# Down products of an adaLN block: eight block products or seven, with the left factors prepared by three engines

## The reference

```python
h = _layernorm(x) * (1 + ca) + sa
x = x + ga * attention(h)                 # linear attention, 16 heads, outside the change
h = _layernorm(x) * (1 + cb) + sb         # x: (2, 2048, 512)
w = lut[idx]                              # gate, up: (1376, 512); down: (512, 1376)
x = x + gb * (silu(h @ gate.T) * (h @ up.T)) @ down.T
```

## Time and profile before

| what | value |
|---|---|
| median of 3 runs | 1165.8 us (1163.17 to 1166.24) |
| span of the profiled execution | 1162.8 us |
| nearest run shown, taken as the profiled execution's own time | 1163.2 us |
| TensorE busy | 1127.7 us, 97% |
| VectorE, ScalarE, GpSimd busy | 705.3, 435.6, 358.1 us |
| last gate and up product to the end of the span | 927.96 to 1162.8 us |

### The profile page before, as it was taken

One profiled execution on the slowest core, in us unless ns is written; L12 is line 12 of the kernel. 1 busy time (PEld: TensorE's weight loads), 2 busy tenths in 40 slices (PEclk: granted clock), 3 DMA queues, 4 the chain that ended last, 5 costly groups with the idle time before them and its releaser, 6 DMA issues.

```text
span 1162.8 us, 16680 instructions
## 1 busy us (share of the span) xinstructions
PE 1127.7 (97%) x6692; PEld 531.1 (46%) x6718; DVE 705.3 (61%) x1035; ACT 435.6 (37%) x729; POOL 358.1 (31%) x331
## 2 busy tenths in 40 slices
PE   4899999999999999999999999999999999999998
PEld 2344444454444444445444444444454444444443
DVE  4788988776779677996768979677432211111111
ACT  4668788776645251424323324233142200000000
POOL 1000100002126283547525637356332211111111
PEclk9999999999999999999999999999999999999999
DMA  7940233113204541312213213031121325445441
GB/s 268 322 135 1 87 109 110 38 37 109 74 1 143 182 145 74 109 73 78 82 35 118 72 72 118 35 118 43 64 92 48 147 104 179 172 173 176 177 154 59
DMA packets 52236, 125.93 MB, mean 108 GB/s; under 512 B 5216, under 2 KB 15456, under 8 KB 47040
## 3 DMA queue, kind: packets, MB, share of 16 engines
q1 hardware_dynamic: 52160, 124.87, 30.9%
HBM read 77.15 MB, written 47.71 MB: 107 GB/s over the span
## 4 chain that ended last, share of the span: by engine, by line
PE 83%; DVE 7%; issue 4%; ACT 3%; POOL 1%; DMA 1%; SPq 0%; POOLq 0%; DVEq 0%; ACTq 0%
PE bank L1232 26%; PE bank L1234 25%; PE bank L1233 25%; PE bank L1240 2%; DVE look_buf L995 2%; PE bank L1384 1%; DVE w_ffn L995 1%; DMA w_ffn<-in_wmod 1%; PE bank L1302 1%; PE bank L1366 1%; PE bank L1345 1%; DVE h L901 1%; ACT h L617 1%; ACT shared L649 1%; DVE shared L1014 0%
## 5 line engine op out<-in xcount | busy, mean ns | idle before, releaser
L1232 PE MATMUL bank<-h,w_ffn 128*128 128x512 f16 (+1 forms) x528 | 200.6, 380 | 0.2 <-POOL h L553 0.2
L1233 PE MATMUL bank<-h,w_ffn 128*128 128x512 f16 (+1 forms) x528 | 200.3, 379 | 0.0
L1234 PE MATMUL bank<-h,w_ffn 128*128 128x512 f16 (+1 forms) x528 | 200.3, 379 | 0.0
L573 POOL TENSOR_TENSOR shared<-hid_f,shared 128x512 f16<-128x512 f32 (+1 forms) x88 | 114.1, 1296 | 273.5 <-ACT shared L780 273.4
L780 ACT ACTIVATE shared<-hid_f 128x512 f16<-128x512 f32 (+1 forms) x88 | 55.4, 630 | 259.7 <-DVE hid_f L1157 251.8
L1164 DVE SCALAR_TENSOR_TENSOR shared<-bank,sc,gb_row 128x512 f32<-128x512 f32 x32 | 24.0, 751 | 205.1 <-PE bank L1234 205.1
L1157 DVE SCALAR_TENSOR_TENSOR hid_f<-bank,sc,shared 128x512 f32<-128x512 f32 (+1 forms) x88 | 65.8, 747 | 121.5 <-issue 82.4
L1232 PE MATMUL bank<-w_ffn 128*128 128x512 f16 x320 | 121.5, 380 | 0.0
L1234 PE MATMUL bank<-w_ffn 128*128 128x512 f16 x320 | 121.3, 379 | 0.0
L1233 PE MATMUL bank<-w_ffn 128*128 128x512 f16 x320 | 121.3, 379 | 0.0
L1232 PE MATMUL bank<-arena,h 128*128 128x512 f16 x256 | 98.3, 384 | 5.6 <-issue 2.5
(11 more groups left out here) (225 smaller groups left out, 1922.8 us busy)
## 6 DMA issues: line engine op xcount, KB each, us to landing
hid_dram<-shared SPq DMA_DIRECT2D x80, 256.0 KB, 2.0
w_ffn<-hid_dram SPq DMA_DIRECT2D x8, 2560.0 KB, 9.5
xg<-in_x SPq DMA_DIRECT2D x16, 1024.0 KB, 7.2
qp_dram<-qp SPq DMA_DIRECT2D x8, 1024.0 KB, 4.9
x_dram<-xg SPq DMA_DIRECT2D x8, 1024.0 KB, 4.0
xg<-x_dram SPq DMA_DIRECT2D x8, 1024.0 KB, 4.8
out<-xg SPq DMA_DIRECT2D x7, 1024.0 KB, 11.4
qp<-qp_dram SPq DMA_DIRECT2D x6, 1024.0 KB, 5.2
```

Source lines behind the costliest of these rows:

```text
L573: pool.tensor_tensor(hid[0:m, e % HIDS, 1], hid_f[0:m, e % 2], hid[0:m, e % HIDS, 0], ALU.subtract).then_inc(hid_done, 1)
L1232: pe.matmul(dst, a_hi, b_hi, start=first, stop=False)
L1233: pe.matmul(dst, a_hi, b_lo, start=False, stop=False)
L1234: last = pe.matmul(dst, a_lo, b_hi, start=False, stop=end)
```

## The change

The down product is made in 16 units of 256 rows. In each, the first 10 chunks and the two halves of 128 rows form a 2 by 2 scheme of blocks (A11, A12, A21, A22, each 5 chunks of 128 by 128), the weights another (5 chunks by 256 columns). In place of 8 block products there are 7 (PRODUCTS), of sums and differences of blocks: on the left S1 = A21 + A22, S2 = S1 - A11, S3 = A11 - A21, S4 = A12 - S2, on the right four T blocks made once. Chunk 11 is added plainly (`rest`).

Gated values go to DRAM in f32. GpSimd makes the four left sums of a unit (`left_sums`), ScalarE all high halves (`left_hi`, `last_hi`), VectorE all low halves (`sum_lo`, `raw_lo`, `last_lo`). ScalarE copies three partial results out of PSUM (`hold`), VectorE combines them (`left_u3`, `out_row`), scales (`out_scale`), and GpSimd adds to `xg` (`add_rows`). In the last step of stage B, VectorE makes the T blocks (`right_sums`, `right_lows`), ScalarE their high halves (`t_hi`), GpSimd the planes of three B blocks and of chunk 11. `hid_hi`, `hid_lo`, `unpack`, `y_tile` go. The core of the diff (constants for scales, views of buffers and semaphore names are left out):

```diff
+HALF_K = (FC - 1) // 2
+HALF_N = HID // 2
+UNIT = 2 * P
+DOWN_UNITS = BATCHES * SEQ // UNIT
...
+PRODUCTS = ((S_A11, S_B11), (S_S1, S_T1), (S_S2, S_T2), (S_A12, S_B21), (S_S3, S_T3), (S_S4, S_B22), (S_A22, S_T4))
+LEFT_PARTS = (S_A11, S_S1, S_S2, S_A12, S_S3, S_S4, S_A22)
...
-        hid = part(shared, 4 * HID, F16, HIDS, 2, GROUP)
+        hid = part(shared, 4 * HID, F32, HIDS, GROUP)
...
+            def hid_load(u):
+                g, i, cols = u // 2, u % 2, slice(u % 2 * UNIT, u % 2 * UNIT + UNIT)
...
+                if u >= 2:
+                    sp.wait_ge(raw_low, 4 * (u - 1))
+                    sp.wait_ge(left_summed, 4 * (u - 1))
+                sp.dma_start(hid_raw[i][:, 0:FC - 1], hid_dram[g][:, 0:FC - 1, cols]).then_inc(hid_in[i], 16)
+                sp.dma_start(hid_raw[i][0:TAIL, FC - 1], hid_dram[g][0:TAIL, FC - 1, cols]).then_inc(hid_in[i], 16)
...
                     elif i == 7:
+                        sp.wait_ge(tf_done, 4 * HALF_K)
+                        sp.wait_ge(b_planes, 3 * HALF_K + 1)
                         hid_load(0)
+                        hid_load(1)
...
+                for u in (2 * g + 2, 2 * g + 3):
+                    if u < DOWN_UNITS:
+                        hid_load(u)
+                if 1 <= g < GROUPS - 1:
+                    sp.wait_ge(stored[1 - par], 16 * ((g - 1) // 2 + 1))
+                    sp.dma_start(flat(xg[:, 1 - par]), x1_dram[g + 1]).then_inc(x1_in[1 - par], 16)
...
+            def b_plane(dst, j, m, cols):
...
+                pool.tensor_copy(dst, down_w[0:m, j, cols].rearrange("p n h -> p h n")).then_inc(b_planes, 1)
+            def right_planes(jj):
+                if jj == 0:
+                    wait_apart(pool, look, len(UNITS) * STEPS)
+                    wait_apart(pool, up_done, SLOT[(GROUPS - 1, 0)] + 1)
+                    b_plane(wt_last[0:TAIL], FC - 1, TAIL, slice(0, HID))
+                b_plane(wt[S_B11][:, jj], jj, P, slice(0, HALF_N))
+                b_plane(wt[S_B21][:, jj], jj + HALF_K, P, slice(0, HALF_N))
+                b_plane(wt[S_B22][:, jj], jj + HALF_K, P, slice(HALF_N, HID))
+            def left_sums(u):
...
+                a11, a12, a21, a22 = r[:, k1, 0:P], r[:, k2, 0:P], r[:, k1, P:UNIT], r[:, k2, P:UNIT]
+                pool.wait_ge(hid_in[u % 2], 32 * (u // 2 + 1))
+                if u:
+                    pool.wait_ge(sum_low, 4 * u)
+                pool.tensor_tensor(left_sum[0], a21, a22, ALU.add).then_inc(left_summed, 1)
+                pool.tensor_tensor(left_sum[2], a11, a21, ALU.subtract).then_inc(left_summed, 1)
+                pool.wait_ge(left_summed, 4 * u + 1)
+                pool.tensor_tensor(left_sum[1], left_sum[0], a11, ALU.subtract).then_inc(left_summed, 1)
+                pool.wait_ge(left_summed, 4 * u + 3)
+                pool.tensor_tensor(left_sum[3], a12, left_sum[1], ALU.subtract).then_inc(left_summed, 1)
+            def add_rows(u, i):
+                g, t = u // 2, 2 * (u % 2) + i
...
+                pool.wait_ge(y_scaled, 2 * u + i + 1)
+                pool.tensor_tensor(xg[:, g % 2, t], xg[:, g % 2, t], y_t[:, i], ALU.add).then_inc(y_done, 1)
...
+            for jj in range(HALF_K):
+                right_planes(jj)
+            left_sums(0)
+            for u in range(DOWN_UNITS):
+                if u:
+                    add_rows(u - 1, 1)
+                if u + 1 < DOWN_UNITS:
+                    left_sums(u + 1)
+                add_rows(u, 0)
+            add_rows(DOWN_UNITS - 1, 1)
...
+            def t_hi(jj):
+                if jj == 0:
...
+                for at, i in enumerate((0, 2, 1, 3)):
+                    act.wait_ge(tf_done, 4 * jj + at + 1)
+                    act.activation(wt[S_T1 + i][:, jj, 0], t_full[:, i], ACT.Copy).then_inc(t_high, 1)
+            def left_hi(u, which):
+                i, pos = u % 2, LEFT_PARTS.index(which)
+                if u >= 2:
+                    act.wait_ge(prod_ready, 7 * (u - 2) + pos + 1)
...
+                if which >= S_S1:
+                    act.wait_ge(left_summed, 4 * u + (0, 2, 1, 3)[which - S_S1] + 1)
...
+                act.activation(left[i][which][:, 0], src, ACT.Copy).then_inc(left_high, 1)
+            def last_hi(u):
+                i = u % 2
+                if u >= 2:
+                    act.wait_ge(prod_ready, 7 * (u - 1))
+                act.activation(left_last[i][0:TAIL, 0], hid_raw[i][0:TAIL, FC - 1], ACT.Copy).then_inc(left_high, 1)
+            def hold(u, k):
+                i = u % 2
+                act.wait_ge(prod_ready, 7 * u + k + 1)
+                if u >= 2:
+                    act.wait_ge(row_out_done, 2 * (u - 2) + 1 if k != 1 else 2 * (u - 2) + 2)
...
+                act.activation(dst, src, ACT.Copy, scale=c1(C_INV_D)).then_inc(row_held, 1)
...
+            stage_b(GROUPS - 1, {jj + 1: [lambda jj=jj: t_hi(jj)] for jj in range(HALF_K)})
+            for which in LEFT_PARTS:
+                left_hi(0, which)
+            last_hi(0)
+            for u in range(DOWN_UNITS):
+                more = u + 1 < DOWN_UNITS
+                if more:
+                    left_hi(u + 1, S_A11)
+                hold(u, 0)
+                if more:
+                    left_hi(u + 1, S_S1)
+                hold(u, 1)
+                if more:
+                    left_hi(u + 1, S_S2)
+                    left_hi(u + 1, S_A12)
+                hold(u, 2)
+                if more:
+                    for which in (S_S3, S_S4, S_A22):
+                        left_hi(u + 1, which)
+                    last_hi(u + 1)
...
+                if e >= HIDS:
+                    dve.wait_ge(hid_out[e % HIDS], 16 * (e // HIDS))
...
+            def right_sums(jj):
...
+                for i in range(2):
...
+                    dve.tensor_tensor(w_full[:, i], words[:, :, 0], words[:, :, 1], ALU.add).then_inc(wf_done, 1)
...
+                dve.wait_ge(wf_done, 2 * jj + 2)
+                dve.tensor_tensor(t_full[:, 0], w1[:, right_n], w1[:, left_n], ALU.subtract).then_inc(tf_done, 1)
+                dve.tensor_tensor(t_full[:, 2], w2[:, right_n], w1[:, right_n], ALU.subtract).then_inc(tf_done, 1)
+                dve.wait_ge(tf_done, 4 * jj + 1)
+                dve.tensor_tensor(t_full[:, 1], w2[:, right_n], t_full[:, 0], ALU.subtract).then_inc(tf_done, 1)
+                dve.wait_ge(tf_done, 4 * jj + 3)
+                dve.tensor_tensor(t_full[:, 3], w2[:, left_n], t_full[:, 1], ALU.subtract).then_inc(tf_done, 1)
+            def right_lows(jj):
+                dve.wait_ge(tf_done, 4 * jj + 4)
+                for at, i in enumerate((0, 2, 1, 3)):
+                    dve.wait_ge(t_high, 4 * jj + at + 1)
+                    ins = dve.tensor_tensor(wt[S_T1 + i][:, jj, 1], t_full[:, i], wt[S_T1 + i][:, jj, 0], ALU.subtract)
+                ins.then_inc(t_low, 1)
+            def sum_lo(u, i):
+                dve.wait_ge(left_high, 8 * u + LEFT_PARTS.index(S_S1 + i) + 1)
...
+                dve.tensor_tensor(block[:, 1], left_sum[i], block[:, 0], ALU.subtract).then_inc(sum_low, 1)
+            def raw_lo(u, which):
+                i = u % 2
+                dve.wait_ge(left_high, 8 * u + LEFT_PARTS.index(which) + 1)
...
+                dve.tensor_tensor(left[i][which][:, 1], src, left[i][which][:, 0], ALU.subtract).then_inc(raw_low, 1)
+            def last_lo(u):
+                i = u % 2
+                dve.wait_ge(left_high, 8 * u + 8)
+                dve.tensor_tensor(left_last[i][0:TAIL, 1], hid_raw[i][0:TAIL, FC - 1], left_last[i][0:TAIL, 0], ALU.subtract).then_inc(raw_low, 1)
+            def left_u3(u):
+                i = u % 2
+                dve.wait_ge(prod_ready, 7 * u + 5)
+                dve.wait_ge(row_held, 3 * u + 2)
+                dve.scalar_tensor_tensor(held_u3[:, i, HALF_N:HID], bank[(0, 6)[i]][:, 0:HALF_N], c1(C_INV_D), held_p5[:, i],
+                                         ALU.mult, ALU.add).then_inc(u3_held, 1)
+            def out_row(u, k):
+                i = u % 2
+                dve.wait_ge(prod_ready, 7 * u + 6 + k)
+                dve.wait_ge(row_held, 3 * u + 3)
+                if u:
+                    dve.wait_ge(y_done, 2 * (u - 1) + k + 5)
...
+                src = bank[(0, 6)[i] if k else (1, 7)[i]]
+                dve.scalar_tensor_tensor(y_t[:, k], src[:], c1(C_INV_D), held_u3[:, i] if k else held_row[:, i],
+                                         ALU.mult, ALU.add).then_inc(row_out_done, 1)
+            def out_scale(u, k):
+                dve.wait_ge(row_out_done, 2 * u + k + 1)
+                dve.tensor_tensor(y_t[:, k], y_t[:, k], gb_row[:, u // (DOWN_UNITS // BATCHES)], ALU.mult).then_inc(y_scaled, 1)
...
+            def right_step(i):
+                if 2 <= i <= HALF_K + 1:
+                    right_lows(i - 2)
+                if 1 <= i <= HALF_K:
+                    right_sums(i - 1)
...
+            def left_part(u, half):
+                if half == 0:
+                    raw_lo(u, S_A11)
```

(72 more changed lines are left out.)

155 lines of the change are left out of this document (74 added, 81 removed).

## The result

Median 1205.82 us of four runs (1204.32 to 1207.62), against 1164.49 for the kernel before (1163.15 to 1166.24): ratio 1.0354, interval 1.0334 to 1.0374. The change makes the kernel slower by 41.3 us. The forecast was 1211 us, and 45.3 more on the profiled execution. That execution's span is 1205.4 us against 1162.8, so 42.6 more.

The account below looks back on a forecast made before the run. TensorE bounds the down stage before the change; afterwards a ring of waits across engines does. Down stage +41.3 and last step of stage B +4 give +45.3: 1208.5 on the profiled 1163.2, 1211 us on the median 1165.8; range 1188 to 1245.

Parts of the forecast that it names:

- the ring: Down stage: cyclic waits through GpSimd sums, ScalarE `hold`, product 4, VectorE and `add_rows` set each unit at 17.05 us.
- TensorE's share: Down stage: 117 matmuls of 256 columns per unit, 0.108 us each with weight loads hidden, 12.64 us against 14.26 before.
- hand-overs: Down-stage unit: six signal delays from one instruction to the next, on the same or another engine, 0.65 us in all.
- the interference of 0.30: Down-stage unit: GpSimd's `add_rows(u,0)` blocks VectorE's `out_scale(u,1)`, 0 to 0.5 us, taken as 0.30.
- the lower bound's price: Down stage: GpSimd sums of 640 elements at 1.53 us each, used for the lowest unit time of 16.0 us.
- the ring does not bind: Rival, down stage: TensorE alone sets the pace, 1141 us; chance 0.05 faster, 0.03 near 14.3 us a unit (same).
- Interference throughout: Rival, down stage: every two-SBUF-input VectorE instruction pays 0.3 and sums cost 1.9; unit 20 us, total 1255, chance 0.14.
- The slow clock: Rival, down stage: TensorE falls to 1.2 GHz, unit 25.3 us, total 1347; chance 0.07 together with other dearer-matmul cases.
- Late loads: Rival, down stage: loads landing in 20 us cost 4.4 on every second unit, +31, total 1242; chance 0.03.
- The last step of stage B: Before the down stage: extra VectorE and ScalarE work, and GpSimd copies, delay TensorE; +4 us, range 0 to 10.
- the removal of `hid_lo`: Before the down stage: dropping this GpSimd work beside a full TensorE gains only small gaps, under 1 us, left out.
- The sum: From the last gate-up matmul to the end: entry 1.9, 15 x 17.05, last unit 12.6, exit 3.1; 273.4 us, +41.3.

Follow-up runs that it names:

- Experiments 5: Changed kernel with product 0 cut to its 5 high-by-high matmuls in place of 15: 1203.73 us, ratio 1.0381.
- 6: Changed kernel with product 4 cut to 5 matmuls in place of 15, and 10 unused matmuls behind each of products 2 and 3: 1192.64 us, ratio 1.0234.
- 7: Changed kernel with one more GpSimd sum of 640 elements per unit, ahead of the others: 1241.99 us, ratio 1.0665.
- 1: Changed kernel with ScalarE copying products 1 and 2 out before making S1, S2 and A12 of the next unit: 1192.46 us, ratio 1.0243.
- 12: Changed kernel with the four left sums per unit moved from GpSimd to VectorE and loads issued earlier: 1151.12 us, ratio 0.9877.
- experiment 11: Changed kernel with holds, GpSimd sums, first row and scale, and loads earlier, plus `left_u3` ahead of the lows of S2 and A12: 1173.65 us, ratio 1.007.
- experiment 10: Changed kernel with only SyncE's loads of gated values issued earlier, engine orders kept: 1204.94 us, ratio 1.035.

## Why the prediction was right

**Direction and place of the ring: right, and its size.** Forecast 17.05, measured 17.02 and 17.08. TensorE's share was right too: matmuls of 256 columns stand 0.109 apart (959.56 to 961.20 has 15 distances), their weight loads of 98 ns hidden, as the earlier trace rows with the earlier trace rows had suggested. The gaps are ahead of products 3 and 4 and end with `hold`. Experiments 5 (TensorE's stream as a whole is not the pace), 6 (product 4 is in the ring), 7 (so are GpSimd's sums), 1 (so is ScalarE's order) and 12 (with the sums off GpSimd the unit is 13.4) show it link by link. The prediction did not see the second branch, over the lows of S2 and A12, which is only 0.85 shorter.

**Inside the ring three terms were off, and cancelled by luck.** By the starts of the timeline above: VectorE 944.32 to 950.77, 6.45; GpSimd to 957.69, 6.92; ScalarE to 959.56, 1.87; product 4 to 961.40, 1.84. My terms with their hand-overs were 6.32 + 0.30 + 0.24 = 6.86; 4.95 + 1.26 + 0.08 = 6.29; 2.10; 1.82. So VectorE was 0.41 and ScalarE 0.23 too high, and GpSimd 0.63 too low. VectorE and ScalarE start the next instruction before the end that the profile gives the last one (lows of 0.82 stand 0.73 apart), which I had not taken off. And I put the interference of 0.30 on one scale alone: it was 0.58 there, 0.51 on the second `add_rows` (1.78 in place of 1.27) and 0.58 on the third sum. That is 1.67 in place of 0.30. In place of 1.65 a sum takes 1.53 undisturbed, which is the lower bound's price. The ring itself was not luck, but that its size came out within 0.03 us was.

**The rivals.** That the ring does not bind fell with the first wait row. Interference throughout (ring of 20) did not happen in the changed kernel, where three instructions of the ring pay for it; it is what experiment 11 ran into when the lows and the sums were laid side by side. The slow clock did come, but only in unit 0: behind a rest that the profile gives as 2.93 us, 15 matmuls of product 3 stood 0.21 apart from 938.5 on. They cost nothing, since product 4 waited for `hold` all the same, 0.40 in place of 2.06 (942.48 below). The rests of 1.92 and 2.06 of later units had no slow matmuls behind them. Late loads were excluded by experiment 10.

**The last step of stage B: the term that failed.** I put +4 on it. The last `hid_full` starts at 928.66, where it was 928.43 before, so the net is +0.2: the last step itself costs 1.9, and 1.7 was gained long before it. The steps of it, in the timeline of the changed kernel:

```profile
875.06 9.37 POOL L600 COPY arena<-w_ffn 96x1024 f16<-96x1024 f16 x16 [18.18 <-PE bank L1432]
...
880.82 4.76 DVE L1281 TENSOR_TENSOR hid_f<-w_ffn 128x512 f32<-128x512 f16 x2
...
888.23 0.75 DVE L1271 SCALAR_TENSOR_TENSOR shared<-bank,sc,shared 128x512 f32<-128x512 f32 x1 [1.06 <-ACT shared L835]
...
890.42 1.29 DVE L1281 TENSOR_TENSOR hid_f<-w_ffn 128x512 f32<-128x512 f16 x2
...
894.36 0.75 DVE L1271 SCALAR_TENSOR_TENSOR shared<-bank,sc,shared 128x512 f32<-128x512 f32 x1 [1.06 <-ACT shared L835]
...
906.73 0.38 PE L1430 MATMUL bank<-h,w_ffn 128*128 128x512 f16 x1 [0.77 <-ACT shared L835]
...
912.75 0.75 DVE L1271 SCALAR_TENSOR_TENSOR shared<-bank,sc,shared 128x512 f32<-128x512 f32 x1 [1.06 <-ACT shared L835]
```

The copies take 0.59 each and block VectorE once, by 4.76 - 1.29 = 3.5 us, which makes that slot 8.1 us long (880.15 to 888.23). The slots after it are 6.13 apart and not 6.95: VectorE's instructions of a slot go by in 5.1 (888.23 to 893.33) and not 5.7, and 1.03 in place of 1.25 stand behind them. So the lag per slot is 0.95 and not 1.8. With the blocked slot it comes to 6.7 at 912.75 (five slots of 5.18 behind 880.15 would be 906.05), where the forecast had 7.1, and TensorE stops twice, 1.6 us in all, where it had 2.4. Without the blocked slot the lag would be 4.8, an estimate; how much of TensorE's stop is the copies' was not tried.

The gain is older. The step before the last ends 1.67 us earlier than it used to (its last `hid_full` at 869.79 and 871.46), and this lead is there from the eighth slot of the first step of stage B on. Up to there TensorE has lost a wait for GpSimd. The kernel before, with GpSimd above and TensorE below the dots:

```profile
405.45 1.46 POOL L573 TENSOR_TENSOR shared<-hid_f,shared 128x512 f16<-128x512 f32 x1 [10.34 <-ACT shared L780]
...
413.84 0.66 PE L1240 MATMUL bank<-ident,arena 128*128 128x128 f32 x4 [1.04 <-POOL arena L548]
```

L573 is `hid_lo`. It stood in GpSimd's list ahead of four instructions (L548) on which TensorE waited until 413.84; in the changed kernel they start 4.15 us earlier (405.22 for 409.37), and TensorE goes on at 412.24 without a wait. So the removal of `hid_lo` was worth most of the 1.7, which I had left out as under 1.

**The sum.** From the end of the gate-up matmuls (928.41) to the end of the last `add_rows` (1201.62 + 1.26 = 1202.88) are 274.5 us, forecast 273.4, before 232.1. The missing 1.1 is all in unit 0, which lasts 18.1 (product 0 of the first two units starts at 930.28 and 948.38) and not 17.05:

```profile
933.97 3.04 POOL L620 TENSOR_TENSOR qp<-w_ffn 128x640 f32<-128x640 f32 x1 [6.80 <-DVE look_buf L1303]
...
942.48 0.27 PE L1743 MATMUL bank<-arena,h 128*128 128x256 f16 x1 [0.40 <-ACT qn_f L875]
```

GpSimd's first sum for unit 1 meets VectorE's lows of unit 0 and takes 3.04 in place of 1.53, and all that follows in the ring comes so much later.

The base of the forecast was off too. It took 1163.2 us as the profiled execution's own time. On record the time of the kernel before is 2.6 to 2.9 above its span, so the span of 1162.8 fits the run of 1165.8 and not that of 1163.2, and 1208.5 was 2.6 too low as the forecast of that execution. The changed kernel's time is only 1.8 above its span, which is most of why the spans are 42.6 apart and the medians 41.3; where that microsecond went is not known.
